# A recommendation tower on one core: the ScalarE program written out for all sixteen groups, the other engines looping over two

## The reference

```python
def _cin_layer(X0, Xi, W, b):
    H = W.shape[0]
    F0_, Fi = (X0.shape[1], Xi.shape[1])
    Wr = W.reshape(H, F0_, Fi)
    return jnp.einsum('hjk,bjd,bkd->bhd', Wr, X0, Xi) + b[None, :, None]

e = jnp.stack([tbl_0[ids[:, 0]], ..., tbl_38[ids[:, 38]]], axis=1)
Xi = X0 = e
for W, b in [(W0, b0), (W1, b1), (W2, b2)]:
    Xi = _cin_layer(X0, Xi, W, b)
    res.append(Xi.sum(axis=2))
h = jnp.concatenate([z, dense_ctx], axis=1)       # z = concatenated res
h = jnp.maximum(h @ W_top1 + b_top1, 0.0)
h = jnp.maximum(h @ W_top2 + b_top2, 0.0)
y = h @ W_top3
```

## Time and profile before

| | us |
|---|---|
| median of 3 runs | 690.02 (689.33 to 690.36) |
| the profiled execution | 693.55 |
| its span, first to last instruction | 691.8 |
| TensorE matmuls busy | 653.7 (94%) |
| DVE busy | 573.9 (83%) |
| ACT busy | 559.8 (81%) |
| GpSimd busy | 359.3 (52%) |

### The profile page before, as it was taken

How to read it: one execution, slowest core, us unless ns; L and a number is a source line. 1 busy time by engine, 2 the same in 40 slices (tenths; PEclk the granted TensorE clock), 3 DMA queues, 4 the chain that set the end, 5 groups by cost and what they waited for, 6 DMA issues and landing times.

```text
span 691.8 us, 11739 instructions
## 1 busy us (share of the span) xinstructions
PE 653.7 (94%) x2662; PEld 482.5 (70%) x2662; DVE 573.9 (83%) x894; ACT 559.8 (81%) x1941; POOL 359.3 (52%) x394
## 2 busy tenths in 40 slices
PE   3688999999999999999999999999999999989898
PEld 2655767777767777677767776777767777767584
DVE  3448788989889999889888988998898989899870
ACT  2339789989879987988878998898799888899762
POOL 7553874655646473738374656647464415132700
PEclk9799999999999999999999999999999999999999
DMA  8115631415041414132321414050414130100000
GB/s 282 19 15 114 156 48 26 94 17 104 9 110 12 108 12 107 16 89 31 76 45 36 85 19 99 8 112 9 109 13 105 13 102 6 58 25 1 1 1 0
DMA packets 67538, 39.65 MB, mean 57 GB/s; under 512 B 58790, under 2 KB 61862, under 8 KB 65348
## 3 DMA queue, kind: packets, MB, share of 16 engines
q1 hardware_dynamic: 60463, 37.71, 23.9%
q0 software_dynamic: 5120, 1.29, 2.2%
q10 hardware_dynamic: 1904, 0.15, 0.2%
HBM read 32.80 MB, written 2.40 MB: 51 GB/s over the span
## 4 chain that ended last, share of the span: by engine, by line
PE 68%; ACT 9%; DVE 9%; issue 8%; DMA 2%; SPq 2%; another core or an unknown queue 1%; ACTq 0%; DVEq 0%
PE yb L992 15%; PE yb L993 15%; PE yb L996 15%; PE p L958 10%; ACT yb L634 7%; PE pq L969 4%; DVE acc L816 3%; DVE x L822 2%; PE yb L910 1%; DVE yb L800 1%; DVE x1l L874 1%; PE yb L1099 1%; PE pq L923 1%; PE p L1071 1%
## 5 line engine op out<-in xcount | busy, mean ns | idle before, releaser
L634 ACT ACTIVATE yb<-yb,x0t 128x128 f32<-128x128 f32 x1728 | 467.7, 377 | 68.8 <-PE yb L996 62.0
L816 DVE TENSOR_TENSOR acc<-acc,yb 128x512 f32<-128x512 f32 (+1 forms) x512 | 324.8, 670 | 45.0 <-ACT yb L634 43.9
L992 PE MATMUL yb<-w1h,x1h 128*128 128x512 f32 (+1 forms) x640 | 310.6, 485 | 13.0 <-DVE acc L816 10.8
L996 PE MATMUL yb<-w1h,x1l 128*128 128x512 f32 (+1 forms) x640 | 247.7, 387 | 0.0
L993 PE MATMUL yb<-w1l,x1h 128*128 128x512 f32 (+1 forms) x640 | 247.5, 387 | 0.0
L427 POOL DMA_INDIRECT emb<-in_table_dram,idx x160 | 152.6, 953 | 50.8 <-issue 38.8
L485 POOL TENSOR_TENSOR late<-late,x0r 117x512 f32<-117x512 f32 (+1 forms) x105 | 132.5, 1296 | 83.9 <-DMA late<-x_scratch 83.7
L992 PEld LDWEIGHTS yb<-w1h,x1h 128*128 128x128 f32 x640 | 120.1, 188 | 78.6 <-DVE acc L816 39.3
L993 PEld LDWEIGHTS yb<-w1l,x1h 128*128 128x128 f32 x640 | 120.6, 188 | 45.0 <-issue 24.8
L996 PEld LDWEIGHTS yb<-w1h,x1l 128*128 128x128 f32 x640 | 120.1, 188 | 25.2 <-DVE x1l L771 0.4
L474 POOL TENSOR_TENSOR bdiag<-mask,x0t 128x312 f32<-128x312 f32 x64 | 45.5, 711 | 152.9 <-PE pq L969 149.6
(11 more groups left out here) (108 smaller groups left out, 328.2 us busy)
## 6 DMA issues: line engine op xcount, KB each, us to landing
late<-x_scratch SPq DMA_DIRECT2D x45, 312.0 KB
late<-x_scratch SPq DMA_DIRECT2D x30, 234.0 KB
emb<-in_table_dram,idx POOLq DMA_INDIRECT x160
gram<-in_L_rec_W_dram SPq DMA_DIRECT2D x1, 2496.0 KB
x_scratch<-x0r SPq DMA_DIRECT2D x15, 156.0 KB
late<-x_scratch SPq DMA_DIRECT2D x15, 156.0 KB
w2t<-in_L_rec_W_dram SPq DMA_DIRECT2D x1, 1280.0 KB
x0t<-embt SPq DMA_DIRECT2D x64, 20.0 KB
```

The costliest lines, as they stand in the source:

```text
L634: op = act.activation(part, part, ACT.Copy, scale=x0t[u][:, t, j:j + 1])
L816: dve.tensor_tensor(part, part, parts(y_bank(t, m), n), ALU.add).then_inc(summed, 1)
L992: pe.matmul(y[:, 0:w], hi, w1h[:, at:at + w], start=True, stop=False)
L996: pe.matmul(y[:, 0:w], lo, w1h[:, at:at + w], start=False, stop=True).then_inc(bank_ready, 1)
```

## The change

ACT's loop over groups 2 to 13 becomes a loop of the program that writes the instructions, so ACT's stream holds all sixteen groups one after the other, with group numbers, semaphore values and addresses as constants. The operations and waits of ACT and their order are the same, as the calls of `period` are. The loops of the other four engines stay as they are.

```diff
@@ -693,7 +693,7 @@
             three_times(1)
             period(0, 0, 0, 2)
             period(1, 0, 1, 2)
-            with act.Fori(1, GROUPS // 2 - 1) as it:
+            for it in range(1, GROUPS // 2 - 1):
                 period(it * 2, it, 0, 2)
                 period(it * 2 + 1, it, 1, 2)
             period(GROUPS - 2, GROUPS // 2 - 1, 0, 1)
```

## The result

| | before | after |
|---|---|---|
| median of runs, us | 690.18 (4 runs) | 680.36 (679.69 to 682.09, 4 runs) |
| ratio, 95% interval | | 0.9864 (0.9844 to 0.9884) |
| the profiled execution, us | 693.55 | 682.09 |
| its span, us | 691.8 | 680.3 |

The changed kernel is 9.8 us faster; 9.14 had been forecast (680.9). In a second session, on another chip, the same two kernels took 692.78 and 681.82: ratio 0.985 (0.9831 to 0.9869).

The account below looks back on a forecast made before the run. TensorE was taken as the bound, kept waiting by ACT's pauses at five loop jumps. Median 690.02 less 9.14 us for the pauses, with 0 for register arithmetic and straight code, gave 680.9 us, range 679.3 to 684.5.

Parts of the forecast that it names:

- What bounds, and the place of the loss: TensorE bounds where not kept waiting; ACT makes it wait at the five jumps back of ACT's loop.
- The five long issue pieces: Stretches of 2.65 to 3.25 us in the chain that ended last, ACT waiting for nothing shown, between loop turns.
- The five pauses, 9.14 us: ACT's pauses at its five jumps back: removing them gains 9.14 us, the five groups' excess over 36.12 us.
- a pause costs its length less 1.2 us: At a group's start, slack hides 1.20 us of each ACT pause; beyond that the loss falls one for one.
- The register arithmetic, 0 of at most 0.7 us: ACT's register instructions in twelve loop groups: removal worth at most 0.7 us, taken as 0.
- The longer straight code, 0: ACT's written-out groups must be fetched while running; taken to cost 0, as existing straight code shows hardly any pauses.
- The profiler's 3.5 us: Profiled execution 3.5 us above the median, place unknown; the 9.14 us gain was taken over whole to the median.
- The rival of a shorter pause without the profiler: All 3.5 us lie in the five passages, so only 5.6 us are won: 684.4 us; chance 0.08.
- No pause moved to another engine: Judges the rival that TensorE, DVE or SyncE pauses instead at its jumps, halving the gain: 685.4 us; chance 0.05.
- The jump was the cause: Judges the rival that pauses stay in straight code and only branch instructions go: 689.8 us; chance 0.02.

Follow-up runs that it names:

- the last experiment: The changed kernel with the loops of SyncE, GpSimd, DVE and TensorE written out as well: 683.09 us, ratio 0.987 to the kernel before.
- 16 fillers: The kernel before with 16 small semaphore instructions near the start of ACT's program, its loop kept: 689.48 us, beside 689.99 for the kernel before.

## Why the prediction was right, point by point

*What bounds, and the place of the loss.* Right. The five long issue pieces, the 3 us of ACT and the five long groups went together, and nothing else moved.

*The five pauses, 9.14 us.* Right in mechanism, 0.4 us too small. The step that was off is the measure: I took group 2's 36.12 us for a group without a pause. It is 36.11 to 36.13 in the kernels after as well. The addition named in the last experiment fits this: the one behind group 2's x1h is still one that DVE has written out, and starts 0.10 us after ACT's scaling, those of groups 3 to 13 are in DVE's loop and start 0.03 us after it; the even groups behind it settle at 36.02 to 36.05. With 36.04 the five excesses are 1.76, 2.00, 2.10, 1.55 and 2.13, or 9.54. That a pause costs its length less 1.2 us was only roughly so where it could be tried again: with 16 fillers the five pauses sum to 13.56 us, and the groups are 9.06 us over 36.04, where 1.20 us off each pause would have given 7.6. Against 36.04 the part of a pause that costs nothing is thus 0.9 us with 16 fillers and 1.1 us in the kernel before (15.15 less 9.54, by five), not 1.20 each time.

*The register arithmetic, 0 of at most 0.7 us.* Right: the seven groups without a pause gave 0.11 us in all, and the loop with its register instructions in place, 48 further on, is as fast as the code without them (681.33 and 681.82 us, on different chips).

*The longer straight code, 0.* Right: no pause at any group, in two profiles.

*The profiler's 3.5 us.* I took the gain over whole, and that held: the medians moved by 9.8 and 11.0 us, the profiled stretch by 9.65. The rival of a shorter pause without the profiler (5.6 us) is refuted. Its premise was a mistake: the 3.5 us needn't be the profiler's at all, for in the second session the profiled execution of the changed kernel (680.16) was the fastest of the four. Where the 3.5 us lay in the one profile of the kernel before isn't shown.

*The other rivals.* No pause moved to another engine: their jumps of 0.2 to 0.3 us stayed. The jump was the cause: the loss falls with the number of jumps, from five to two to none, and it goes with all five in place where each takes 0.3 us. But the reason that I gave for it was wrong in one point. I wrote that the engine with the long body pays. It is the place of the body against the blocks that are fetched, length only sets how many places are good. DVE's loop with the 274 instructions was free because of where it happened to stand, and 64 instructions ahead of it made the changed kernel 26 us slower. The prediction didn't need this, as code without a loop has no place to be wrong in.

## What to carry to other kernels

Ask the loop line of each engine for the time from its compare-and-branch to its next instruction: here 0.3 us was a free jump, and 3 to 5 us one that fetched. A dear one can be removed by writing the loop out, which was free of pauses in every run here, or by moving the loop some tens of instructions, which costs nothing here but has to be looked at again after every edit ahead of the loop. And an edit that only adds instructions ahead of a loop can cost 26 us for a reason that has nothing to do with what it adds: before blaming the edit, look at the jumps, and then at the granted clock of the groups behind them.

## What the runs showed of the hardware that was not expected

The same loop body costs 0.3 us or 3.8 to 5.1 us per jump on ACT, and 0.3 or 4.3 to 4.9 us on DVE, by its place alone. The good places for 312 instructions are fewer than 96 wide in a row, and come between two bad ones 128 apart. The four-group loop on DVE, with its 547 instructions too long for three blocks of 128, paid less per jump (2.9 and 3.2 us) than the badly placed short one, and the one on ACT, 4.2 and 4.0 us, lies at the low end. DVE's stops of 2.9 to 3.4 us cost more than their length, since behind them TensorE's granted clock fell for a while, and that was up to 9.9 of the 25.8 us.
